# Both layer norms' rows moved from VectorE to ScalarE, and the projection's bias from VectorE to GpSimd

## The reference

```python
x = x + tanh(g_xattn) * attention(layernorm(x), ctx, ctx)      # output projection: out @ Wo + bo
x = x + tanh(g_ffn)   * experts(layernorm(x))                  # routed by softmax(logits), top 2; plus the shared expert

def _layernorm(x, axis=-1, eps=1e-05):
    m = jnp.mean(x, axis=axis, keepdims=True)
    v = jnp.var(x, axis=axis, keepdims=True)
    return (x - m) / jnp.sqrt(v + eps)
```

## Time and profile before

| What | us |
|---|---|
| median of 3 runs (lowest, highest) | 598.15 (596.72, 605.92) |
| the profiled execution, its own time | 592.66 |
| its span | 591.0 |
| PE busy, share of the span | 530.8 (90%) |
| DVE busy | 372.7 (63%) |
| ACT busy | 241.0 (41%) |
| POOL busy | 230.5 (39%) |

### The profile page before, as it was taken

How to read it: one execution, slowest core, us unless ns; L and a number is a source line. 1 busy time by engine, 2 the same in 40 slices (tenths; PEclk the granted TensorE clock), 3 DMA queues, 4 the chain that set the end, 5 groups by cost and what they waited for, 6 DMA issues and landing times.

```text
span 591.0 us, 12133 instructions
## 1 busy us (share of the span) xinstructions
PE 530.8 (90%) x3143; PEld 461.2 (78%) x3144; DVE 372.7 (63%) x771; ACT 241.0 (41%) x528; POOL 230.5 (39%) x177
## 2 busy tenths in 40 slices
PE   4915999868899869999999999999999999999995
PEld 3615888858888758888888888888888888888884
DVE  3463577787768468666655566555655556555888
ACT  2203556454556443343344343433334333343431
POOL 8032225341500006774415443444444444301773
PEclk9957788897989869999999999999999999999999
DMA  7776355653576222324667665736776667111453
GB/s 237 184 207 206 96 152 161 211 165 94 147 226 215 90 97 99 124 107 142 188 205 203 211 188 183 225 115 204 200 237 178 216 175 224 48 37 55 136 175 122
DMA packets 75421, 95.86 MB, mean 162 GB/s; under 512 B 6469, under 2 KB 63236, under 8 KB 75404
## 3 DMA queue, kind: packets, MB, share of 16 engines
q0 software_dynamic: 23712, 57.18, 32.0%
q1 hardware_dynamic: 44316, 32.44, 18.2%
q10 hardware_dynamic: 7376, 6.03, 3.5%
HBM read 68.15 MB, written 20.71 MB: 150 GB/s over the span
## 4 chain that ended last, share of the span: by engine, by line
PE 60%; POOL 10%; DVE 9%; issue 9%; DMA 5%; ACT 4%; SPq 1%; DVEq 1%; POOLq 0%; ACTq 0%
PE ps L645 13%; PE ps L632 7%; PE ps L633 7%; PE ps L634 7%; PE ps L646 7%; PE ps L620 6%; POOL gath L564 5%; POOL routed_x L528 5%; PE ps L702 3%; PE ps L688 3%; PE ps L659 2%; PE ps L613 2%; DMA moved_q<-hid 1%; DMA qstack<-moved_q 1%; DVE xres L1126 1%
## 5 line engine op out<-in xcount | busy, mean ns | idle before, releaser
L645 PE MATMUL ps<-w2hl,hTh 128*128 (+1 forms) x440 | 161.6, 406 | 2.9 <-DVE hTl L1142 2.9
L646 PE MATMUL ps<-w2hl,hTl 128*128 (+1 forms) x440 | 123.6, 281 | 0.0
L992 ACT ACTIVATE hid<-hid 128x512 f32<-128x512 f32 x110 | 69.3, 632 | 131.5 <-DVE hid L1148 131.4
L645 PEld LDWEIGHTS ps<-w2hl,hTh 128*128 128x128 f32 x440 | 82.7, 188 | 20.4 <-issue 3.5
L986 ACT ACTIVATE hTh<-ps 128x512 fp32r<-128x512 f32 x110 | 60.0, 597 | 94.4 <-PE ps L620 94.4
L1148 DVE TENSOR_TENSOR hid<-ps,b1bc 128x512 f32<-128x512 f32 x110 | 75.3, 689 | 29.7 <-PE ps L634 24.7
L632 PE MATMUL ps<-w1l,xT 128*128 (+1 forms) x220 | 92.5, 420 | 0.0
L633 PE MATMUL ps<-w1h,xT 128*128 (+1 forms) x220 | 87.5, 398 | 0.0
L634 PE MATMUL ps<-w1h,xT 128*128 (+1 forms) x220 | 87.2, 396 | 0.0
L646 PEld LDWEIGHTS ps<-w2hl,hTl 128*128 128x128 f32 x440 | 83.0, 189 | 0.0
L1142 DVE TENSOR_TENSOR hTl<-ps,hTh 128x512 fp32r<-128x512 f32 x110 | 70.8, 685 | 0.2
(11 more groups left out here) (160 smaller groups left out, 782.0 us busy)
## 6 DMA issues: line engine op xcount, KB each, us to landing
stage<-in_L_ffn_W POOLq DMA_DIRECT2D x16, 1024.0 KB, 6.1
w1h<-in_L_ffn_W POOLq DMA_DIRECT2D x8, 1024.0 KB, 5.8
w2hl<-in_L_ffn_W POOLq DMA_DIRECT2D x8, 1024.0 KB, 7.9
qstack<-moved_q SPq DMA_DIRECT2D x48, 128.0 KB, 2.4
xrow<-routed_x SPq DMA_DIRECT2D x39, 128.0 KB, 2.1
routed_y<-yrow ACTq DMA_DIRECT2D x39, 128.0 KB, 1.7
routed_x<-zeros SPq DMA_DIRECT2D x6, 768.0 KB, 3.9
moved_q<-hid SPq DMA_DIRECT2D x16, 256.0 KB, 2.3
```

What stands on the lines that cost most here:

```text
L645: mm(p_y, hTh[:, c, :], part(2 * D), start=c == 0, stop=False)
L646: last = mm(p_y[:, 0:D], hTl[:, c, :], part(D), start=False, stop=c == FC - 1)
L992: act.activation(hid[:, n, :], hid[:, n, :], ACT.Gelu).then_inc(S["h_act"], 1)
```

## The change

- ScalarE's new `normal(t)` writes `xn` as rstd * x + nmr, with a scale and an offset for each row, in place of VectorE's `norm_in`. The offset `nmr` = -mean * rstd is one more instruction of `newton` for each of its two parts. In the loop `normal(t + 4)` stands after the exponent and ahead of the deviation.
- ScalarE's `deviation` gets three instructions: the negated mean, the offset of the row (both one column), and the row `x2row` itself, in place of VectorE's `norm_two`.
- GpSimd multiplies `bo_bc` by tanh(g) once and adds it to x, two tiles at a time, after each key product (`add_bo`). It waits for `xn_ready` of both tiles, as the norm needs x without the bias. The residual waits for `bo_added`, and its second instruction is gone.
- ScalarE's loop form ends one step earlier, with that step written out.

```diff
--- before.py
+++ after.py
@@ -189,7 +189,8 @@
         mv2 = a("mv2", [P, 2])
         lnv2 = a("lnv2", [P, 1])
         r2 = a("r2", [P, 1])
-        nw2 = a("nw2", [P, 4])
+        nw2 = a("nw2", [P, 6])
+        nmr = a("nmr", [P, NT])
         x2row = a("x2row", [P, D])
         x2T = a("x2T", [P, C, P])
         attn.close()
...
@@ -483,33 +484,52 @@
             pool.wait_ge(S["sel_set"], 1)
             pool.wait_ge(S["k_stacked"], 16 * 2 * (P // ROWS))
             pool.wait_ge(S["k_stacked_act"], 16 * (P // ROWS))
+            pool.wait_ge(S["gate_tanh"], 1)
+            pool.wait_ge(S["bo_in"], 16)
+            pool.tensor_tensor(bo_bc[:], bo_bc[:], tgate[:, 0:1].to_broadcast([P, D]), ALU.mult).then_inc(S["bo_scaled"], 1)
+
+            def add_bo(b):
+                t0 = TB * b
+                pool.wait_ge(S["bo_scaled"], 1)
+                pool.wait_ge(S["xn_ready"], t0 + TB)
+                pool.tensor_tensor(xres[:, t0:t0 + TB, :], xres[:, t0:t0 + TB, :],
+                                   bo_bc[:].unsqueeze(1).to_broadcast([P, TB, D]), ALU.add).then_inc(S["bo_added"], 1)
+
             key_diag(0)
+            add_bo(0)
             key_diag(1)
+            add_bo(1)
             pool.wait_ge(S["x_in1"], 16)
             pool.wait_ge(S["v_ps"], B // 2)
             load_b1(0, shared_b[0])
             load_b2(0, shared_b[1])
             load_w1(0, sW1_v)
             key_diag(2)
+            add_bo(2)
             load_hi1(0, sW1_v)
             load_w2(0, sW2_v)
             key_diag(3)
+            add_bo(3)
             load_hi2(0, sW2_v)
             split_w1(0, 0)
             ready_1(0)
             key_diag(4)
+            add_bo(4)
             load_w1(1, expert_w1(0))
             split_w2(0, 0)
             ready_2(0)
             key_diag(5)
+            add_bo(5)
             load_w2(1, expert_w2(0))
             load_b1(1, expert_b(0)[0])
             load_b2(1, expert_b(0)[1])
             load_hi1(1, expert_w1(0))
             key_diag(6)
+            add_bo(6)
             load_hi2(1, expert_w2(0))
             split_w1(1, 1)
             key_diag(7)
+            add_bo(7)
             load_w1(2, expert_w1(1))
             ready_1(1)
             split_w2(1, 1)
@@ -871,6 +891,14 @@
                 act.wait_ge(S["ln_log"], part + 1)
                 act.activation(rstd[:, t0:t1], lnv[:, t0:t1], ACT.Exp, scale=-0.5).then_inc(S["ln_rstd"], 1)
 
+            def normal(t):
+                if isinstance(t, int):
+                    act.wait_ge(S["ln_newton"], 5 if t < FIRST else 10)
+                if not isinstance(t, int) or t >= 1:
+                    act.wait_ge(S["xnT_ps"], t)
+                act.activation(xn[:], xres[:, bass.ds(t, 1), :].rearrange("p o d -> p (o d)"), ACT.Identity,
+                               bias=nmr[:, bass.ds(t, 1)], scale=rstd[:, bass.ds(t, 1)]).then_inc(S["xn_ready"], 1)
+
             def norm_in(t, bank=p_wo):
                 act.wait_ge(S["xnT_ps"], t + 1)
                 act.activation(xnT[:].rearrange("p c q -> p (c q)"), bank, ACT.Copy).then_inc(S["xnT_sb"], 1)
@@ -917,6 +945,7 @@
                 act.activation(lnv2[:], mv2[:, 1:2], ACT.Ln, bias=eps[:, 0:1]).then_inc(S["ln2_log"], 1)
                 act.activation(nw2[:, 0:1], mv2[:, 1:2], ACT.Identity, bias=neg_eps[:, 0:1], scale=-0.5
                                ).then_inc(S["nw_a"], 1)
+                act.activation(nw2[:, 4:5], mv2[:, 0:1], ACT.Copy, scale=-1.0).then_inc(S["nw_e"], 1)
                 act.wait_ge(S["ln2_log"], t + 1)
                 act.activation(r2[:], lnv2[:], ACT.Exp, scale=-0.5).then_inc(S["r2_done"], 1)
                 act.wait_ge(S["r2_done"], t + 1)
@@ -927,6 +956,17 @@
                                ).then_inc(S["nw_c"], 1)
                 act.wait_ge(S["nw_c"], t + 1)
                 act.activation(nw2[:, 3:4], nw2[:, 2:3], ACT.Copy, scale=r2[:, 0:1]).then_inc(S["nw_d"], 1)
+                met(act)
+                act.wait_ge(S["nw_d"], t + 1)
+                met(act)
+                act.wait_ge(S["nw_e"], t + 1)
+                act.activation(nw2[:, 5:6], nw2[:, 3:4], ACT.Copy, scale=nw2[:, 4:5]).then_inc(S["nw_f"], 1)
+                if not isinstance(t, int) or t >= 1:
+                    act.wait_ge(S["x2_out"], 16 * t)
+                    act.wait_ge(S["x2T_ps"], t)
+                act.wait_ge(S["nw_f"], t + 1)
+                act.activation(x2row[:], xres[:, bass.ds(t, 1), :].rearrange("p o d -> p (o d)"), ACT.Identity,
+                               bias=nw2[:, 5:6], scale=nw2[:, 3:4]).then_inc(S["x2_ready"], 1)
 
             def step(t):
                 ok = lambda u: not isinstance(t, int) or 0 <= u < NT
@@ -947,6 +987,8 @@
                     queries(t + 3)
                 if ok(t + 1):
                     exponent(t + 1)
+                if ok(t + 4):
+                    normal(t + 4)
                 if ok(t - 1):
                     deviation(t - 1)
 
@@ -955,17 +997,21 @@
             deviations(0, 0, FIRST)
             for m in range(C, 2 * C):
                 keys_hi(m)
+            normal(0)
             norm_in(0, p_in)
             act.wait_ge(S["bq_in"], 16)
             queries(0)
             act.wait_ge(S["k_zero"], 1)
             for g in range(P // ROWS):
                 act.dma_start(stacked(2, g), keys_of(0, g)).then_inc(S["k_stacked_act"], 16)
+            normal(1)
             norm_in(1, p_in)
             queries(1)
+            normal(2)
             norm_in(2, p_in)
             queries(2)
             deviations(1, FIRST, NT)
+            normal(3)
             act.wait_ge(S["v_zero"], 1)
             act.wait_ge(S["v_sb"], B // 2)
             for j, pair, h, key, to, n in SEGMENTS:
@@ -975,8 +1021,8 @@
             exponent(0)
             step(0)
             step(1)
-            each(act, 2, NT - 3, step)
-            for t in range(NT - 3, NT + 2):
+            each(act, 2, NT - 4, step)
+            for t in range(NT - 4, NT + 2):
                 step(t)
 
 
@@ -1063,7 +1109,7 @@
 
             def newton(part, t0, t1):
                 dve.wait_ge(S["ln_rstd"], part + 1)
-                n = 4 * part
+                n = 5 * part
                 tt(nw[:, 0, t0:t1], rstd[:, t0:t1], rstd[:, t0:t1], ALU.mult).then_inc(S["ln_newton"], 1)
                 dve.wait_ge(S["ln_newton"], n + 1)
                 stt(nw[:, 1, t0:t1], mv[:, t0:t1, 1], EPS, nw[:, 0, t0:t1], ALU.add, ALU.mult
@@ -1073,18 +1119,13 @@
                 dve.wait_ge(S["ln_newton"], n + 3)
                 tt(rstd[:, t0:t1], rstd[:, t0:t1], nw[:, 2, t0:t1], ALU.mult).then_inc(S["ln_newton"], 1)
                 dve.wait_ge(S["ln_newton"], n + 4)
+                stt(nmr[:, t0:t1], mv[:, t0:t1, 0], -1.0, rstd[:, t0:t1], ALU.mult, ALU.mult).then_inc(S["ln_newton"], 1)
 
             def col(ap, t):
                 return ap[:, bass.ds(t, 1)]
 
             def row(ap, t):
                 return ap[:, bass.ds(t, 1), :].rearrange("p o d -> p (o d)")
-
-            def norm_in(t):
-                if not isinstance(t, int) or t >= 1:
-                    dve.wait_ge(S["xnT_ps"], t)
-                ts(xn[:], row(xres, t), row(mv, t)[:, 0:1], col(rstd, t), ALU.subtract, ALU.mult
-                   ).then_inc(S["xn_ready"], 1)
 
             def queries_lo(t):
                 dve.wait_ge(S["q_hi"], t + 1)
@@ -1121,11 +1162,12 @@
             def residual(t):
 
                 dve.wait_ge(S["wo_ps"], t + 1)
+                if not isinstance(t, int):
+                    met(dve)
+                dve.wait_ge(S["bo_added"], t // TB + 1)
                 stt(row(xres, t), p_wo, tgate[:, 0:1], row(xres, t), ALU.mult, ALU.add).then_inc(S["x1_mid"], 1)
+                met(dve)
                 dve.wait_ge(S["x1_mid"], t + 1)
-                stt(row(xres, t), bo_bc[:], tgate[:, 0:1], row(xres, t), ALU.mult, ALU.add).then_inc(S["x1_done"], 1)
-                met(dve)
-                dve.wait_ge(S["x1_done"], t + 1)
                 dve.bn_stats(st2[:], row(xres, t)).then_inc(S["st2_done"], 1)
                 met(dve)
                 dve.wait_ge(S["st2_done"], t + 1)
@@ -1149,21 +1191,12 @@
                        b1bc[:, bass.ds(s, 1), n * (F // 2):(n + 1) * (F // 2)].rearrange("p o f -> p (o f)"),
                        ALU.add).then_inc(S["h_add"], 1)
 
-            def norm_two(t):
-                dve.wait_ge(S["nw_d"], t + 1)
-                if not isinstance(t, int) or t >= 1:
-                    dve.wait_ge(S["x2_out"], 16 * t)
-                    dve.wait_ge(S["x2T_ps"], t)
-                ts(x2row[:], row(xres, t), mv2[:, 0:1], nw2[:, 3:4], ALU.subtract, ALU.mult).then_inc(S["x2_ready"], 1)
-
             def keep_logits(t):
                 dve.wait_ge(S["l_ps"], t + 1)
                 dve.tensor_copy(row(logits, t), p_l).then_inc(S["l_sb"], 1)
 
             def step(t):
                 ok = lambda u: not isinstance(t, int) or 0 <= u < NT
-                if ok(t - 2):
-                    norm_two(t - 2)
```

(7 more changed lines are left out.)

4 lines of the change are left out of this document (2 added, 2 removed).

## The result

Over 20 runs each, the changed kernel has a median of 599.66 us (594.13 to 607.71) and the kernel before 599.09 (593.0 to 605.92). The ratio of the times is 1.0072, 95% interval 1.0045 to 1.0100: the change costs up to 0.7%, some 4.3 us, where I had forecast a gain of 7.5. The ratio and its interval leave out runs in the chip's slower state, while the medians are over all runs and differ by 0.1% alone. So it is sure that the gain did not come, and the size of the loss is less sure than its interval says.

What follows compares the result with a forecast made beforehand. It took the attention loop's path through VectorE's residual and bias, ScalarE's chain and TensorE's queue as what the change can affect; +6.3 - 6.0 - 15.8 + 8.5 - 0.5 = -7.5 gave 590.7 us as median, range 578 to 604.

Steps and rivals of the forecast that it cites:

- within 2%: Whole kernel: time changes by less than 12 us either way, between 586.2 and 610.1; chance 0.66.
- Turns longer: Attention loop: ScalarE's longer chain, less VectorE's bias, adds 0.57 us a turn, +6.3 over eleven turns.
- The norm of x hidden on ScalarE: Attention loop: the norm's 0.6 us a turn hides behind the exponent, where ScalarE waits anyway; 6.6 if not.
- The locks go: Attention loop: VectorE's waits for GpSimd in two long turns end; all 15.8 us of disturbances are counted off.
- The start: Before the loop: moved loads close a hole, -6.5, later spread transfers cost +0.5; -6.0 us together.
- the hole closes: Before tile 2's scores: the 5.05 us hole goes and scores run at full clock; -6.5 us.
- rival 2: Start gives nothing: moved loads meet spread transfers, later exponent eats the hole; -1.5, 596.7 us; chance 0.10.
- New disturbances (a): Attention loop: seven bursts of moved weight loads delay the queries' loads; 4.5 us.
- R+2.0: Attention loop: weight loads predicted to start 2.0 us after R, the start of a turn's residual on VectorE.
- rival 3: Attention loop: queries' load becomes the wait, disturbances 24 instead of 8.5; +8, 606 us; chance 0.13.
- (b): Attention loop: TensorE idles more, so four of eleven turns get a clock dip at 1.0 each; 4 us.
- The end of the loop: End of loop: VectorE's logits copy no longer stands behind L1157, but ScalarE's row is 0.35 later; net -0.5 us.

Runs made afterwards that it cites:

- The kernel with only the waits: Kernel before, with only GpSimd's waits for the first norm of each pair's second tile added behind key products; no add or norm moved: 618.70 us, ratio 1.0393.
- the two-buffer version: Changed kernel with two buffers for the second norm's row, so ScalarE need not wait for the last row's transfer: 598.34 us, ratio 1.0014.
- the row behind the copy: Kernel with GpSimd's adds behind the weight loads and splits, with the second norm's offset and row on ScalarE moved behind copy L904: 586.56 us, ratio 0.9826.
- the adds behind the loads: Changed kernel with GpSimd's order alone altered: each add but the first moved behind the weight loads and splits it stood ahead of: 590.83 us, ratio 0.9903.

## Why the prediction was wrong

I said 590.7 with 0.66 for "within 2%"; the measured ratio means about 602.5 on the scale of the 598.15 that I started from. That is inside the range but on the wrong side of no change. By its steps:

- **Turns longer: right.** 9.05 us (9.1 predicted). From L958 to L904 are 1.39 us, where 0.31 were; with the negated mean and less the bias's 0.51 the copy is 0.66 later (0.55 predicted), and the turn 0.53 longer. Alone, the row makes +1.0 (9.53). L733 waits 1.06 to 1.5 for the copy, as listed.
- **The norm of x hidden on ScalarE: right** in the loop. The turn of 8.54 in its own experiment shows it.
- **The locks go: right in the changed kernel**, where no VectorE instruction is over 1.2 us. But I had argued from the operands of the rows and never asked where the splits go. The kernel with only the waits shows them moved onto VectorE's row, 3.9% slower. The change escapes this because the row left VectorE with it. The first norm's row alone ends the long lock as well, so part of these locks was the chance of where a turn stood.
- **The start, -6.0: the step that failed first.** It measured +0.3. I had put +0.5 (0 to 2.6) on ScalarE's spread transfers; they start 3.8 later, the exponent behind them comes 4.5 later, and SyncE's last spread transfer, which I had not looked at, lands after 7.28 beside the moved load L388. I had read "the hole closes" as a gain. But a hole in front of scores is a gain only if what comes before it does not move, and it moved by 3.2 us (first attention at 53.97, before 50.74). This was my rival 2, with 0.10.
- **New disturbances (a), 4.5: the right mechanism, too small.** I had the loads just ahead of the queries' loads at R+2.0 (measured 2.10), and priced the 2 MB burst at 1 and the 2.6 MB burst at 2. They cost 4.84 and 4.97, by landings of 9.62 and 10.98 us. I had worked out that a landing of 11.0, the worst of the earlier trace rows, overruns by nearly 5, and kept that price for rival 3. (That worst one lies before the loop, at 34.42, beside the spread transfers and the load L387.) The single loads were priced about right: two waits of 0.96 and 0.99, and none of the turns that hold them is longer for it. Of the slow turns of (b), 4 in my sum, two came, both behind the large waits: the two turns with these waits are 12.7 over, 9.8 of it the waits and 2.9 what followed, with a granted clock of 0.50 from 83 to 89 and from 144 to 149. All excess in the loop is 12.9 against my 8.5. That is most of rival 3, which decides where a landing is over 6.3 us; it happened twice, not four times.
- **The end of the loop, -0.5: wrong in sign.** I had looked at VectorE's logits copy, which did come free (at 182.70 it no longer stands behind a row), and not at where the last weight load would stand. It was 0.66 us ahead of the queries' write, which then took 7.4 us, and TensorE stood still for 2.24. In the profiled execution the last four tiles are 11.0 longer, most of it at a granted clock of 0.50. The row's own wait for its buffer, which I had not priced either, is there too; the two-buffer version bounds it at about half a per cent. How much of the 11.0 is the change's stays open.

Summed against the traces: loop 2.8 where my terms gave +6.3 - 15.8 + 8.5 = -1.0; start +0.3 where I had -6.0; end +12.0 where I had -0.5. Of the last I can't say how much is the change's and how much this execution's clock. By the ratios, the place of the loads is the step that decided: moved back, the same work is 1.7% faster than the changed kernel and 1.0% faster than before. It costs because the adds stand in front of something, not because of their own time.

The Trainium skill, DMA: Bandwidth & Descriptors, section "Queues, rings and completion order", has an engine take turns between queues by packets. As I read it, that would at most double a small transfer behind a load. This case's landings went from 2.4 to 9.62 and 10.98 us; the measurement decides, and I was right not to follow the page but too timid in my price.

The Trainium skill, SBUF — State Buffer, section "SBUF: two separate sides", says that VectorE's two-port operations and GpSimd's hold the shared ports for a whole instruction while the other waits. The traces agree: 4.50 us beside a split of 4.51, and 2.47 beside a key product of 2.26. It names no place in a program; that a wait of GpSimd's picks which VectorE instruction is caught is what the kernel with only the waits showed (four rows of 4.33 to 4.62 us, where the kernel before has one of 4.50).

Open: what the row behind the copy gained by, since its turns did not shorten; why the low clock lasted so long in the last tiles of the profiled execution; and how much of the loss over many runs is the start's and how much the row's length. I tried no version in which the weight loads are split into smaller transfers, which would tell the size of a burst from its place.

## What to carry to other kernels

When work is put into a queue with a new wait in it, list what stands behind that wait and ask what those instructions will now meet, in time and not only in order: here a shift of 2 us in a load's place against the turn was worth 2.7% with the bias moved alone and 1.7% in the whole change, more than any of the three parts by itself. Take the worst landing seen for a load just behind a burst as its price, not the median, and look at every small transfer of the path, the write as well as the loads. A hole that closes is a gain only if the work before it has not moved, so read the start of what comes before the hole too.

## What of the hardware was not expected

- **A small transfer behind a megabyte.** The queries' loads, 128 KB each on SP's queue, land in 2.4 us (median). They took up to 9.62 and 10.98 where GpSimd had issued a 1 MB weight load 0.08 and 0.47 us ahead and issued another within the next 1.6 us. Near single loads (issued at 94.65, 112.79 and 156.28) they took up to 4.9, 6.0 and 7.0, and the waits were 1 us or none, since the turn has the room. The queries' write (2.3 median) took 7.4 at 180.94, 0.66 behind a load, and with the adds behind the loads still 8.2 at 118.75, 3 us behind the last load of a burst. A store of the second norm's row, also 128 KB, took 7.53 behind the load of 174.40; a transfer of zeros stands ahead of it in the same queue, but behind the same zeros and with no weight load near it took 3.8 in the kernel before.
- **A VectorE row can be caught for longer than the GpSimd instruction.** 5.55, 5.38 and 5.59 us with splits of 4.51: the row started with GpSimd's issue of the load ahead of the split (91.13 and 91.09) and was held through both.
- **Ten transfer issues hold ScalarE for 8.64 to 9.35 us** in its own order, so a norm ahead of them is paid by everything behind them.
- **ScalarE's row of 256 columns with scale and offset per row takes 0.60 us** in all 16 tiles of the changed kernel, beside a split of GpSimd's too. I had 0.6 from a slope of 0.87 ns a column.
